# The MLP of a two-layer kernel over rows taken in blocks of 128 across sequence borders instead of 112 within them

## The reference

```python
attn_out = attn_out @ out_w + out_b + residual
out = rmsnorm(attn_out, postnorm_w)
out = jax.nn.gelu(out @ mlp_w1 + mlp_b1) @ mlp_w2 + mlp_b2
return out + residual
```

## Time and profile before

| | |
|---|---|
| device time, median of 3 runs | 954.01 us (953.47 to 956.18) |
| the profiled execution | 956.08 us |
| its span | 954.4 us |
| TensorE matmul busy | 893.8 us, 94% of the span |
| VectorE, ScalarE, GpSimd busy | 558.3, 423.7, 231.7 us |
| mean granted clock of TensorE | 0.983 of full speed |

### The profile page before, as it was taken

The page is one execution under the profiler, slowest core; times in us unless marked ns, Lnnn a source line. Parts: engine busy times, 40 slices in busy tenths (PEclk is TensorE's granted clock), DMA queues, the critical chain, the costliest instruction groups (busy, mean ns, idle before and its releaser), DMA issues.

```text
span 954.4 us, 17633 instructions
## 1 busy us (share of the span) xinstructions
PE 893.8 (94%) x6888; PEld 695.8 (73%) x6888; DVE 558.3 (59%) x1286; ACT 423.7 (44%) x957; POOL 231.7 (24%) x243
## 2 busy tenths in 40 slices
PE   4767999999999989999999999999999889999998
PEld 3656777677677765667777787878777667888886
DVE  3398999999999897343323232333333447445444
ACT  3212342424333534426565565665656673333331
POOL 3455556465546394000000000000000002001000
PEclk9978999999999998999999999999999999999999
DMA  8756455463736433006010101010100240002001
GB/s 273 162 154 175 110 151 154 140 152 107 199 88 178 121 86 97 27 1 255 9 52 8 52 9 53 9 52 9 53 8 10 90 147 1 1 0 70 8 0 39
DMA packets 40602, 78.95 MB, mean 83 GB/s; under 512 B 17805, under 2 KB 23949, under 8 KB 38734
## 3 DMA queue, kind: packets, MB, share of 16 engines
q1 hardware_dynamic: 40526, 77.91, 28.5%
HBM read 68.72 MB, written 9.18 MB: 82 GB/s over the span
## 4 chain that ended last, share of the span: by engine, by line
PE 46%; issue 4%; ACT 2%; DVE 2%; DMA 0%; POOL 0%; DVEq 0%; ACTq 0%; POOLq 0%
PE bank L1719 9%; PE bank L1596 8%; PE bank L1707 7%; PE bank L1590 6%; PE bank L1611 4%; PE bank L1670 4%; PE bank L1662 3%; PE bank L1692 3%; ACT smb L1210 2%; PE bank L1625 2%; PE bank L1680 1%; DVE smb L860 0%; PE bank L1346 0%; DVE lt_lo L875 0%; DMA lat_in<-lat_scratch 0%
## 5 line engine op out<-in xcount | busy, mean ns | idle before, releaser
L860 DVE CUSTOM_DVE_ANT_0 smb<-bank,mask 112x487 f32<-112x487 f32 x128 | 78.6, 660 | 111.3 <-issue 111.3
L645 DVE TENSOR_TENSOR_SCAN scan<-bank,scan 128x448 f32<-128x448 f32 x128 | 132.3, 1076 | 10.1 <-POOL scan L502 10.1
L1352 PEld LDWEIGHTS bank<-xj,front 128*128 128x128 f32 x1024 | 121.2, 198 | 16.2 <-issue 10.7
L1352 PE MATMUL bank<-xj,front 128*128 128x112 f32 x1024 | 123.6, 282 | 7.4 <-POOL xj L490 7.4
L499 POOL TENSOR_TENSOR scan<-scan,ks 128x896 f32<-128x896 f32 x64 | 124.0, 1938 | 10.5 <-DMA scan<-v_scratch 10.1
L1210 ACT ACTIVATE smb<-smb,nmax 112x487 f32<-112x487 f32 x128 | 88.4, 692 | 81.7 <-DVE nmax L860 81.7
L476 POOL TENSOR_TENSOR small<-small,neghalf 112x1 f32<-112x1 f32 x24 | 14.2, 592 | 397.2 <-DVE small L884 302.9
L652 DVE TENSOR_TENSOR scan<-scan,bank 128x896 f32<-128x896 f32 x64 | 69.1, 1082 | 0.8
L490 POOL TENSOR_TENSOR xj<-tmp,xa 128x448 f32<-128x448 f32 x40 | 42.4, 1062 | 86.1 <-DVE tmp L614 86.1
L1670 PE MATMUL bank<-ident,smb 112*122 112x112 f32 x512 | 58.0, 261 | 0.8
L1218 ACT COPY pts<-bank 122x448 f32<-122x448 f32 x128 | 58.3, 542 | 0.0
(11 more groups left out here) (181 smaller groups left out, 1867.1 us busy)
## 6 DMA issues: line engine op xcount, KB each, us to landing
scan<-v_scratch SPq DMA_DIRECT2D x64, 448.0 KB, 5.5
cx<-in_ctxt SPq DMA_DIRECT2D x8, 750.0 KB, 4.9
raw_w<-in_wbig SPq DMA_DIRECT2D x4, 1024.0 KB, 8.1
w<-in_w SPq DMA_DIRECT2D x1, 4096.0 KB, 14.4
w<-in_w SPq DMA_DIRECT2D x2, 2048.0 KB, 8.2
v_scratch<-vt SPq DMA_DIRECT2D x64, 56.0 KB, 1.9
tail<-in_wbig SPq DMA_DIRECT2D x3, 1024.0 KB, 11.0
front<-in_wbig SPq DMA_DIRECT2D x2, 1024.0 KB, 10.6
```

Of the source, the lines that this page charges most:

```text
L645: n = v.tensor_tensor_scan(flat, decay, flat, 0.0, ALU.mult, ALU.add)
L860: v.tensor_tensor_reduce(sm[r], bank[r][0:T, 0:NKEY], mask_b[b % 2][:, :], -1.0 / DH, 3e38, ALU.add, ALU.min, nmax[:, h:h + 1]).then_inc(s ...
L1352: i = t_.matmul(tiles(dst)[:, m, :], w[:, k, m * P:(m + 1) * P], x[:, k, :], start=k == 0, stop=k == NT - 1)
```

## The change

The 896 rows are no longer taken as eight sequences of 112 but as seven blocks of 128 rows, regardless of where a sequence ends. Pass 0 covers rows 0 to 511 (four blocks), pass 1 rows 512 to 895 (three blocks). h1 and its parts lie as [128, k, 896], so that the columns of a pass are contiguous. A hidden product has 12 matmuls of 512 columns in pass 0 and of 384 in pass 1; an output product has 12 matmuls in pass 0 and 9 in pass 1, of 512 columns each as before, with 128 rows as the stationary operand. The gelu and its split work on 512 and 384 columns. The parts in which h1 is split are rows 0 to 223, 224 to 511 and 512 to 895; the second needs five sequences instead of four. The latents, b2 and the result are moved in blocks of 128 rows: seven stores, and three reloads after pass 0 instead of four. ACT's one loop over the steps becomes two, one for each pass.

```diff
-BC = 4
+ROWS = B * T
+BLOCKS = (4, 3)
+PASS_AT = (0, 4 * P)
+PASS_ROWS = (4 * P, ROWS - 4 * P)
+NB = sum(BLOCKS)
+H1_PARTS = ((0, 2 * T, 2), (2 * T, 4 * P, 5), (4 * P, ROWS, B))
...
-        h1 = room_t.take("h1", [P, B, NT, T])
+        h1 = room_t.take("h1", [P, NT, ROWS])
...
# SP: after each y2_ready, a store; after pass 0, the reload
-                sp.dma_start(out[b], lat_all[:, b % BC, :]).then_inc(s[f"out_stored{b % BC}"], 16)
-                if b < BC:
+                sp.dma_start(out_rows[j * P:(j + 1) * P], lat_all[:, m, :]).then_inc(s[f"out_stored{m}"], 16)
+                if j < BLOCKS[1]:
...
# DVE
-            def h1_low(n, first, last):
-                dve.wait_ge(s["h1_hi_ready"], n)
-                v.tensor_tensor(h1_lo[:, first:last], h1[:, first:last],
-                                h1_hi[:, first:last].bitcast(F32), ALU.subtract).then_inc(s["h1_lo_ready"], 1)
+            def h1_low(n):
+                first, last, _ = H1_PARTS[n]
+                dve.wait_ge(s["h1_hi_ready"], n + 1)
+                v.tensor_tensor(h1_lo[:, :, first:last], h1[:, :, first:last],
+                                h1_hi[:, :, first:last].bitcast(F32), ALU.subtract).then_inc(s["h1_lo_ready"], 1)
...
-                v.tensor_copy(hid_hi[p][:, :], hid[p][:, :]).then_inc(s["hid_hi_ready"], 1)
+                v.tensor_copy(hid_hi[p][:, 0:w], hid[p][:, 0:w]).then_inc(s["hid_hi_ready"], 1)
...
-                    v.tensor_tensor(buf, bank[OUT_BANK[b % BC]][0:T, :], buf, ALU.add).then_inc(s["y2_ready"], 1)
+                    v.tensor_tensor(buf, bank[OUT_BANK[j]][:, :], buf, ALU.add).then_inc(s["y2_ready"], 1)
...
# ACT
-            def h1_high(first, last):
-                act.wait_ge(s["h1_ready"], last)
-                c_.copy(h1_hi[:, first:last], h1[:, first:last]).then_inc(s["h1_hi_ready"], 1)
+            def h1_high(n):
+                first, last, sequences = H1_PARTS[n]
+                act.wait_ge(s["h1_ready"], sequences)
+                c_.copy(h1_hi[:, :, first:last], h1[:, :, first:last]).then_inc(s["h1_hi_ready"], 1)
...
-            with act.Fori(2, NF - 1) as i:
-                step(act.snap(2 * i), 0)
-                step(act.snap(2 * i + 1), 1)
+            with act.Fori(2, NF // 2) as i:
+                step(0, act.snap(2 * i), 0)
+                step(0, act.snap(2 * i + 1), 1)
+            with act.Fori(NF // 2, NF - 1) as i:
+                step(1, act.snap(2 * i), 0)
+                step(1, act.snap(2 * i + 1), 1)
...
# PE
-                        i = t_.matmul(bank[HID_BANK[p]][:, 0:BC * T], w[:, k, :], x[:, n * BC:(n + 1) * BC, k, :],
+                        i = t_.matmul(bank[HID_BANK[p]][:, 0:PASS_ROWS[n]], w[:, k, :],
+                                      x[:, k, PASS_AT[n]:PASS_AT[n] + PASS_ROWS[n]],
...
-                for b in range(BC):
+                for j in range(BLOCKS[n]):
                     if n and start:
-                        pe.wait_ge(s["y2_ready"], b + 1)
+                        pe.wait_ge(s["y2_ready"], j + 1)
                     for x, w in ((xh, wh), (xh, wl), (xl, wh)):
-                        i = t_.matmul(bank[OUT_BANK[b]][0:T, :], x[:, b * T:(b + 1) * T], w[:, :],
+                        i = t_.matmul(bank[OUT_BANK[j]][:, :], x[:, j * P:(j + 1) * P], w[:, :],
```

More of the change, by code:

```diff
@@ L210, in build @@
             at = room.at
-            hid.append(room.take(f"hid{i}", [P, BC * T]))
-            hid_lo.append(view(f"hid_lo{i}", at, [P, BC * T], F32R))
-        hid_hi = [room.take(f"hid_hi{i}", [P, BC * T], F32R) for i in range(2)]
+            hid.append(room.take(f"hid{i}", [P, 4 * P]))
+            hid_lo.append(view(f"hid_lo{i}", at, [P, 4 * P], F32R))
+        hid_hi = [room.take(f"hid_hi{i}", [P, 4 * P], F32R) for i in range(2)]
         b1v = room.take("b1v", [P, NF])
@@ L217, in build @@
         w2_lo = [room.take(f"w2_lo{i}", [P, C], F32R) for i in range(2)]
-        lat_all = room.take("lat_all", [T, BC, C])
+        lat_all = room.take("lat_all", [P, BLOCKS[0], C])
         b2_rows = ob_rows
@@ L568, in _ @@
             pool.wait_ge(s["b2_loaded"], 16)
-            for b in range(B):
-                pool.wait_ge(s[f"lat_back{b % BC}"], 16 * (b // BC + 1))
-                g.tensor_tensor(lat_all[:, b % BC, :], lat_all[:, b % BC, :], b2_rows[:, :], ALU.add
+            for j in range(NB):
+                m = j % BLOCKS[0]
+                pool.wait_ge(s[f"lat_back{m}"], 16 * (j // BLOCKS[0] + 1))
+                g.tensor_tensor(lat_all[:, m, :], lat_all[:, m, :], b2_rows[:, :], ALU.add
                                 ).then_inc(s["latb2_ready"], 1)
@@ L918, in attention @@
                 else:
[L919 to L920 removed]
+                    h1_low(0)
+                    h1_low(1)
                     w1_low(0, 0, 0)
@@ L1303, in attention, with hidden @@
                     act.wait_ge(s["b1_loaded"], 16)
-                    hidden(0, 0, first=True)
+                    hidden(0, 0, 0, first=True)
                 keep_inverse(b)
-            def hidden(g, p, first=False):
+            def hidden(n, g, p, first=False):
+                w = PASS_ROWS[n]
                 act.wait_ge(s["hp_ready"], g + 1)
@@ L1318, in _, with step @@
             w2_high(1, 1)
-            def step(g, p, first=False, last=False):
-                hidden(g, p, first)
+            def step(n, g, p, first=False, last=False):
+                hidden(n, g, p, first)
                 if not last:
```

103 lines of the change are left out of this document (53 added, 50 removed).

## The result

| | before | after |
|---|---|---|
| median of six runs of each; those of before include the three that gave 954.01 (us) | 957.18 (953.47 to 959.64) | 945.52 (943.45 to 952.30) |
| profiled execution (us) | 956.08 | 951.20 |
| its span (us) | 954.4 | 949.5 |
| PE busy (us), matmuls | 893.8, 6888 | 887.1, 6840 |
| PE busy, share of span | 94% | 93% |

A forecast was written before the change was run, and what follows sets the result against it. PE's columns were taken to bound the MLP passes. The terms -11.1 + 4.6 - 5.3 + 0.3 + 0.5 + 0.24 + 0.1 gave -10.6 us, from the median 954.01 to 943.4 us, range 941.0 to 946.4.

The forecast's parts named there:

- item 6: Waits in the MLP passes: the two split stalls of 0.7 us in pass 0 keep their length, 0 us (-0.2 to 0).
- Item 1: Output products: 384 matmuls become 336 at an unchanged 0.2317 us each, -11.1 us.
- The rival of the full stationary operand: Output matmuls with 128 stationary rows take 128/112 of their time, +11.1 us, so no change at 954.5 us; 2%.
- Items 2 and 3: Hidden products: pass 0's 512 columns cost +4.6 us behind the entrance and +0.3 in last attention; pass 1's 384 save 5.3.
- The weight loads: Rival: loads of 128 columns pace pass 1's 384-column matmuls at 0.192 us each, +2.9 us, 946.3 us; 5%.
- Items 4 and 5: Last attention: h1's larger second part, +0.5 us; MLP second-half entrance: gelu, cast and subtraction on 512 columns, +0.24 us.
- Item 7: Turn of the passes and end: additions unchanged, one reload less, last store 256 instead of 224 KB, +0.1 us (0 to +0.37).
- the rival that made DVE the pace: Pass 1: DVE, slowed beside POOL's additions, sets the step time, costing 24 us, 967 us; 3%.
- a real case: DVE slowed in pass 1 only beside POOL's three additions at its start, costing 1 or 2 us.
- The clock rival: Idle times in last attention and at the entrance bring one more clock fall of 3.4 us: +1.7 us, 945.1 us; 9%.

The follow-up runs named there:

- experiment 6: Changed kernel with POOL's b2 additions delayed, plus the 48 output matmuls saved in pass 1 issued again: 955.95 us, ratio 1.0005 to the kernel before.
- experiment 1: The changed kernel run once more, no edit, beside the kernel before: median 946.96 us against 954.95, ratio 0.9915.
- experiment 4: Kernel before, unedited, run again: 955.15 us; changed kernel with POOL adding b2 on only 112 partitions: 948.2 us (one run each).
- experiment 5: Kernel before with POOL's b2 additions on 128 partitions: 960.59 us; changed kernel with each addition waiting for the last to complete: 943.62 us (one run each).
- experiment 2: POOL's b2 additions wait until the splits of eight steps are done, in both kernels: before 954.31 us (ratio 0.999), changed 943.31 us (ratio 0.987).
- after_again: The changed kernel run once more with no edit: median 946.96 us, ratio 0.9915 to the kernel before.
- after_late: Changed kernel with POOL's b2 additions waiting until the splits of eight steps are done: 943.31 us, ratio 0.987 to the kernel before.
- before_late: Kernel before with POOL's b2 additions waiting until the splits of eight steps are done: 954.31 us, ratio 0.999 to the kernel before.
- after_late_order: Changed kernel with delayed b2 additions and last attention reordered (h1's first part three sequences, row scaling before second subtraction): 940.44 us, ratio 0.9833 to the kernel before.
- before_wide: Kernel before with POOL's b2 additions on 128 partitions instead of 112: 960.59 us in one run, the kernel before 952.8 beside it.
- after_112: Changed kernel with POOL adding b2 on partitions 0 to 111 only, leaving it out of 16 rows per block: 948.2 us in one run.
- after_late_twelve: Changed kernel with delayed b2 additions, pass 1's third output block computed twice (48 matmuls put back): 955.95 us, ratio 1.0005 to the kernel before.

## Why the prediction was right, and where it was wrong

The main mechanism was right: PE's columns set the time of the passes, and 48 output matmuls fewer give about 11 us (experiment 6). One step failed, the wait in item 6, which was put at nothing and is 2.2 us. The median lies in the range all the same, partly because the end of the kernel gave 0.7 us back, and partly by luck: the interval of the gain, 5.8 to 13.3 us, is wider than the miss. The profiled execution, with 4.9 us gained instead of 10.6, shows the miss and adds two falls of the clock.

| item | forecast | measured | from |
|---|---|---|---|
| 1. output products | -11.1 | -10.4 | 32 x 2.775 before; 16 x 2.80 and 16 x 2.10 after |
| 2 and 3. hidden products behind the entrance | -0.7 | -0.7 | 30 x 2.447 before; 14 x 2.79 and 16 x 2.105 after |
| 2, 4, 5. in the last attention and at the entrance | +1.0 | +0.9 | second stretch, 355.0 and 355.9 |
| 6. waits in the passes | 0 | +2.2 | 2.9 instead of 0.7 |
| 7. end | +0.1 | -0.6 | fourth stretch |

*Item 1.* An output matmul with 128 stationary rows takes 0.2333 us (2.80 / 12), not 0.2317: I had read the equality off matmuls of 122 rows. The rival of the full stationary operand, which gave them a seventh more, came true by under one per cent, 0.5 us; with the rounding of the 0.2317 of before the item is 0.7 us short. Experiment 6 shows the item as a whole: give the 48 back and the gain is zero.

*Items 2 and 3.* 384 columns take 0.1754 us (2.105 / 12), in proportion to 448 (0.1750), where I took 0.1767 off a line. What that saves, 0.2 us, goes again in pass 0, whose hidden products take 2.79 us instead of 2.78. The Trainium skill, "TensorE: Matmul & The Clock Gate", section "Wait — 56ns, not 53.3ns?", has a rule that makes 162.5 ns for 384 columns, as an estimate; the trace has 175. The weight loads (0.19 us in the profile) don't pace the 384 columns: that rival falls.

*Items 4 and 5.* DVE's subtraction on 1152 elements took 1.36 us and ACT's cast 1.14, as forecast; PE idled 3.24 us before the transposes (forecast 3.3) and 2.26 at the entrance (2.3):

```profile
764.94 0.60 PE L1363 MATMUL bank<-ident,rows_y 112*128 112x112 f32 x4 [3.24 <-DVE rows_y L899]
```

The second stretch holds one fall of 3.4 us before and one after, so the 0.9 us are the edit's own in this pair.

*Item 6 is the step that failed.* It reads: "The two stalls of 0.7 us in pass 0 keep about their length, since chain and cover grow alike: 0 (ends -0.2 and 0)". The cover was counted right, and the chain was not: I counted the gelu, the cast and the subtraction, all of which grew by a seventh, and not what stands ahead of the split in DVE's queue, the row scaling beside POOL's additions. It takes 5.2 us instead of 1.5, and the wait is 2.9 us instead of 0.7 (experiments 1, 4 and 5). Item 7 passes over the additions at the turn of the passes because they "have the same 512 elements a partition"; POOL's, which the prediction costs nowhere in pass 0, had 16 partitions more. Where I looked at the conflict, in the rival that made DVE the pace, I looked at pass 1, where it costs nothing: the windows there show DVE 14.61 of 20 us busy beside three additions, with PE at 20.00:

```profile
880.00:900.00 20.00, 20.00 (x103) 18.13 (x102) 14.61 (x23) 7.47 (x13) 4.37 (x3) 1.00 0.29 93
```

The rival's price for "a real case", 1 or 2 us, was right to a factor of two. Its place was not.

*Item 7.* From the start of the last output matmul to the end of the span 3.7 us instead of 4.3. The page, part 6, which answers to the earlier trace rows:

```profile
out<-lat_all SPq DMA_DIRECT2D x7, 256.0 KB, 2.0
```

256 KB over 128 partitions land in 2.0 us, in all eight profiles that store such blocks; 224 KB over 112 took 2.6 to 2.7 in the four others. I had scaled by the bytes. Why the larger store is quicker no run here tells.

*The sum.* -10.6 as forecast, +0.7 (item 1), +2.2 (item 6), -0.7 (item 7) and -0.1 (items 2, 4, 5): -8.5 us, which from 954.01 gives 945.5. The ratio gives 944.5 (940.7 to 948.2), and the median of after is 945.52; that it meets the sum so closely is chance. The 11 and 22 runs of experiment 1 give 8.1 us (4.9 to 11.4). For the profiled pair add 3.0 to 3.3 us for the two falls of the clock and 0.5 for the later start of the second layer: 4.7 to 5.0 us gained, against 4.9 measured. With the additions moved out of the way, item 6 becomes a gain and the change is worth 11.0 us (experiment 2).

*The clock rival.* It gave one more fall, 1.7 us, and had 9%. In the profiled execution there are two more, at the entrance and behind the new stall. `after_again` has the same idle times and neither of them, `after_late` none in that stretch, and `before_late`, which has the entrance of before, has one there. So the falls come with idle times of 2 to 3 us and not after each of them. But counted over all profiles, from the first scores to the first steps behind the entrance, the rival did better than its 9%. The granted clock was at 0.50 for 6.8 us in each of the seven profiles with the changed kernel's order in the last attention: 3.4 us there and 3.4 behind the entrance, or all 6.8 in the last attention (`after_again`, `after_late`). Of the four profiles with the order of before, three had 3.4 us and one, `before_late`, 6.8. `after_late_order`, with an idle time of 0.69 us instead of 3.29, had 3.4. Where the second fall lies in the last attention, that stretch is 1.3 and 1.5 us longer (357.1 and 357.3 against 355.9). Behind the long stall came a further fall in two of its three profiles (`after`, and `before_wide` with 6.8 us). With one or two executions of each kernel, and no run in which only the idle time changes, it is likely and not shown that the change brings one fall more. The Trainium skill, "TensorE: Matmul & The Clock Gate", section "Part 1: The HAM clock gate (the "warmup" mystery)", has the half clock as the default that activity lifts; that leaves open why one execution falls and the other does not, and so do these runs. The profiled execution of after, 951.2 us, was the one with two falls and a late start of the second layer; the 5.7 us by which it lies over its kernel's median say little of the change.

*Not settled.* The second layer's first scores start between 422.8 and 430.2 us in the profiles, and no kernel here changes what lies ahead of them. That is as much as the spread of the runs; no experiment looked at it. The traces show a part of the cause: over the first 400 us the granted clock is 0.98 on average where the start is earliest (422.80, `after_again`), and 0.96 and 0.95 in the two with the latest (430.23, `after_112`, and 430.17, `after_late_twelve`). It is not all, since at 0.97 the starts still lie anywhere from 424.6 to 429.1.

## What to carry to other kernels

When a tile goes from 112 to 128 partitions, go through every instruction on it, on the idle engines too, and see what each runs beside: the time of an instruction alone may stay while what it does to its neighbour triples. When you cost a wait, follow the late engine's queue back past the chain that you know, up to the instruction that last had to wait. Work that nobody needs soon (here POOL's additions of a bias) is safest behind a wait of its own, in a stretch where the other engine has time.

## What the runs showed of the hardware

DVE's row scaling (one tensor in, 112 x 512) takes 0.49 us alone; 1.50 to 1.51 us beside POOL's additions on 112 partitions, or on 128 with a wait after each; and 5.19 to 5.22 us, until all four are done, beside four additions on 128 partitions without a wait between them. The two-input subtractions take 1.59 to 1.78 us beside either height of addition, instead of 0.62 to 0.69 alone. The cast of the split, with one input too, takes 0.38 to 0.42 us beside the additions and 0.38 to 0.43 alone, so one input alone does not make an instruction slow there. The lengths fit turns: four additions last 5.0 us where DVE is kept out and 6.3 to 6.5 where its instructions come in behind the first three.

The Trainium skill, "SBUF — State Buffer", section "🔬 SBUF: two separate sides", calls the port pair that the two engines share an exclusive lock, held "for the whole instruction" by whichever started first. The 1.5 us agree: one addition, 5.0 / 4 = 1.25 us, and some of the scaling's own time. The 5.2 us do not: there the loser waited for four instructions. What hands the turn over, why 16 partitions or a wait decide it, and which trait of the scaling matters, was not found; only 112 and 128 partitions were tried, and the scaling always started 0.07 us behind the first addition or clear of them all.
